# Transformer stage: q/k parts stored one by one and fetched in one transfer of 48 partitions, three head groups normalised early, q's rotation and splitting moved to VectorE

## The reference, cut to what matters

```python
NL, D, H, DFF = (6, 128, 16, 512)   # HD = 8
def _rope(x):      # x1*cos - x2*sin, x1*sin + x2*cos on the two halves of each head
def _attn(q, k, v, mask):
    scores = jnp.einsum('bqhd,bkhd->bhqk', q, k) / np.float32(np.sqrt(HD))
    scores = jnp.where(mask[:, None, None, :], jnp.float32(-jnp.inf), scores)
    w = jax.nn.softmax(scores, axis=-1)
    return jnp.einsum('bhqk,bkhd->bqhd', w, v)
```

## Time and profile before

| | |
|---|---|
| median of 3 runs | 5220.8 us (5213.22 to 5223.22) |
| the profiled execution | 5205.5 us, span 5203.7 us |
| PE busy | 4381.7 us (84%) |
| DVE busy | 3406.6 us (65%) |
| ACT busy | 2302.0 us (44%) |
| POOL busy | 504.0 us (10%) |
| mean granted TensorE clock | 0.879 |

### The profile page before, as it was taken

The page is one execution under the profiler, slowest core; times in us unless marked ns, Lnnn a source line. Parts: engine busy times, 40 slices in busy tenths (PEclk is TensorE's granted clock), DMA queues, the critical chain, the costliest instruction groups (busy, mean ns, idle before and its releaser), DMA issues. The chain is left out here.

```text
span 5203.7 us, 88732 instructions
## 1 busy us (share of the span) xinstructions
PE 4381.7 (84%) x25098; PEld 2768.5 (53%) x25446; DVE 3406.6 (65%) x17506; ACT 2302.0 (44%) x7385; POOL 504.0 (10%) x420
## 2 busy tenths in 40 slices
PE   8999999999999987587787878778733697997979
PEld 6888888888888865223333333333322453333456
DVE  7888888888888876455555555555434594433535
ACT  4555555555555543263545454545422122332313
POOL 0000000000000001111221212222101001222000
PEclk9999999999999988697878787878765698998769
DMA  0000000000000001302222222221100010000001
GB/s 27 2 2 2 2 2 2 2 2 2 2 2 2 2 8 43 51 14 34 38 35 38 34 38 34 37 35 30 18 5 3 14 35 24 9 8 10 19 1 37
DMA packets 89492, 91.41 MB, mean 18 GB/s; under 512 B 21311, under 2 KB 84442, under 8 KB 88811
## 3 DMA queue, kind: packets, MB, share of 16 engines
q1 hardware_dynamic: 89067, 86.46, 8.6%
HBM read 70.22 MB, written 15.39 MB: 16 GB/s over the span
## 5 line engine op out<-in xcount | busy, mean ns | idle before, releaser
L287 DVE CUSTOM_DVE_ANT_0 I-219junk<-I-215encw,I-218expo,I-227rec 128x77 f32<-128x77 f32 x3072 | 941.1, 356 | 5.8
L1307 DVE TENSOR_REDUCE I-41381nmax<-ps 128x1 f32<-128x512 f32 x768 | 498.3, 686 | 235.7 <-PE ps L975 225.6
L1195 ACT ACTIVATE I-41384prob<-ps 128x512 f32<-128x512 f32 x768 | 428.6, 594 | 247.5 <-remote 135.4
L265 ACT ACTIVATE I-217tanh_s<-ps 128x77 f32<-128x77 f32 x1024 | 242.4, 237 | 593.9 <-PE ps L245 593.9
L245 PE MATMUL ps<-I-212hist,I-49small 128*128 128x77 f32 x2048 | 456.5, 304 | 40.6 <-DVE I-212hist L323 40.4
L245 PEld LDWEIGHTS ps<-I-212hist,I-49small 128*128 128x128 f32 x2048 | 304.9, 188 | 296.8 <-DVE I-212hist L323 296.7
L251 PE MATMUL ps<-I-217tanh_s,I-49small 128*128 128x77 f32 x2048 | 454.7, 304 | 0.0
L975 PE MATMUL ps<-I-41375kS,I-41374qS 96*128 96x512 bf16 x768 | 347.4, 479 | 111.4 <-DMA I-41374qS<-parts 53.3
L252 PE MATMUL ps<-I-212hist,I-49small 128*128 128x128 f32 x2048 | 440.0, 297 | 0.0
L247 PE MATMUL ps<-I-212hist,I-216uh_h 128*128 128x128 f32 x2048 | 439.8, 296 | 0.0
L273 ACT ACTIVATE I-223hh<-I-229gate_t,I-228pre,I-222rh 128x1 f32<-128x1 f32 x1024 | 395.5, 386 | 84.6
(11 more groups left out here) (494 smaller groups left out, 7980.0 us busy)
## 6 DMA issues: line engine op xcount, KB each, us to landing
I-41374qS<-parts SPq DMA_DIRECT2D x144, 128.0 KB
parts<-I-41393room SPq DMA_DIRECT2D x36, 384.0 KB, 2.5
I-41375kS<-parts SPq DMA_DIRECT2D x72, 128.0 KB
I-49small<-in_layers SPq DMA_DIRECT2D x6, 768.0 KB, 19.2
I-41374qS<-I-41383mrow SPq DMA_DIRECT2D x192, 2.0 KB
I-41374qS<-I-41390crow SPq DMA_DIRECT2D x192, 2.0 KB
I-41393room<-in_own SPq DMA_DIRECT2D x5, 387.0 KB, 4.0
I-41368wk<-in_own SPq DMA_DIRECT2D x6, 320.0 KB, 12.8
```

Of the source, the lines that this page charges most:

```text
L287: return e.tensor_tensor_reduce(junk[:, 2 * g + b, :], encw[:, g, b, :], expo[:, b, :], inv[:, b:b + 1], rec[:, b, g:g + 1], ALU.mult, ALU ...
L1195: e.activation(prob[:, tau % 2, j, :], k.ps[:, b, :], ACT.Exp, scale=scale).then_inc(free[b], 1)
L1307: e.tensor_reduce(nmax[:, U % HG, i, j:j + 1], k.ps[:, use[0], :], AX.X, ALU.max, negate=True).then_inc(free[use[0]], 1)
```

## The change

1. **Layout.** `qS`, `kS`, `cS` become (partition, batch entry, head, token), so that 16 heads of one entry lie together in a partition. The columns of the k, q, cross-k and cross-q weights are reordered on GpSimd (`by_dim`) from head-major to dimension-major into new tiles `wk_d` and `wq_d`, and `cos` and `sin` are reloaded in that order by 8 DMAs in the setup stage.
2. **Stores and fetch.** The DRAM buffer holds six rows of parts per job. Each part is stored as soon as it is made, in its own DMA, to all the rows that hold it (high 3, middle 2, last 1). One DMA of 48 partitions by 16 KB fetches all six rows. The wait is 48 for stores and 16 for the fetch.
3. **Normalisation.** The sum is taken over groups 0 to 2 only, after which these three are normalised; group 3 gets a reciprocal of its own, of its own `o`. GpSimd multiplies only group 1. The same for the cross attention (`cinv`, `co_in`).
4. **q on VectorE.** `join`, `rest_part` and `last_part` of `q` and `cq` move from GpSimd to VectorE; those of `k` and `ctx` stay.
5. Semaphores of the two halves of `part3` are apart, in SP's stream the jobs `ctx` and `cq` stand ahead of the weight loads, and all tables of `TURNS` are written anew.

```diff
-    vector=("rrrrrrrrmmmmmmmmmmmmmmmmmmmmmmmmmmmmmmmmmmmmm...
+    vector=("rrrrrrrmmmmmmmmmmmmmmmmrmmmmmmrmmmmmmmmmrmmmmm...
...
-        qS = sbuf(ctx, nc, "qS", [ROWS_ALL, NH, B * T], BF16)
+        qS = sbuf(ctx, nc, "qS", [ROWS_ALL, B, NH, T], BF16)
...
-        parts_dram = nc.dram_tensor("parts", (4, 3, P, T), BF16).ap()
+        parts_dram = nc.dram_tensor("parts", (4, 6, P, T), BF16).ap()
...
-                e.wait_ge(s.own, 16 * 2)
+                at = offsets(SMALL)[0]["cos"][0]
+                for d in range(8):
+                    e.dma_start(small[16 * d:16 * d + 16, at:at + 2 * T], small_dram[d:P:8, at:at + 2 * T]).then_inc(s.own, 16)
+                e.wait_ge(s.own, 16 * 10)
...
+        Q_SPOTS = (slice(0, 3), slice(4, 6), slice(3, 4))
+        K_SPOTS = (slice(2, 5), slice(1, 6, 4), slice(0, 1))
...
                             if m == 0 and n == 0:
-                                e.wait_ge(s.jsent3, 96 * (a + 1))
-                                e.wait_ge(s.jsent2, 96 * (a + 1))
+                                e.wait_ge(s.jsent3, 16 * (a + 1))
+                                e.wait_ge(s.jsent2, 16 * (a + 1))
...
                 def attend(a):                                  # vector
-                    e.wait_ge(s.pooled, 3 * (a + 1))
-                    e.reciprocal(inv[:], inv[:]).then_inc(s.inv, 1)
-                    yield
                     for n in range(HG):
                         U = HG * a + n
-                        e.wait_ge(s.inv, a + 1)
+                        if n == 0:
+                            e.wait_ge(s.pooled, 2 * (a + 1))
+                            e.reciprocal(inv[:], inv[:]).then_inc(s.inv, 1)
+                            yield
+                        if n == HG - 1:
+                            e.wait_ge(*done(values(a, n)))
+                            e.wait_ge(s.wide, U)
+                            e.reciprocal(inv[:], o[:, n, :]).then_inc(s.inv, 1)
+                        e.wait_ge(s.inv, 2 * a + 1 + n // (HG - 1))
...
-                        if n % 2 == 0:
+                        if n != 1:
...
                         turn_pair("tx", "txs", 1, T)            # vector; the same behind qx, qxs for "cq"
+                        join("q", "tx", "txs", 1, T)
+                        yield
+                        rest_part("q", 1, T)
+                        yield
+                        last_part("q", 1, T)
                         yield
...
+                    def by_dim(dst, src, ready):                # gpsimd
+                        e.tensor_copy(dst[:, 0:512].rearrange("p (n d h) -> p n d h", n=4, d=8),
+                                      src[:, 0:512].rearrange("p (n h d) -> p n d h", n=4, d=8)).then_inc(ready, 1)
...
-                    def store(name, n, m):                      # sync
+                    def store(name, n, m, which, spots):
                         spot = SPOT[name]
-                        e.wait_ge(s.last, job[r, name])
-                        if times(r, name) > 1:
-                            e.wait_ge(jsent[spot], 96 * (times(r, name) - 1))
-                        e.dma_start(parts_dram[spot, :, :, 0:m].rearrange("r p t -> p r t"),
-                                    part3[:, n, :, 0:m]).then_inc(jstored[spot], 16)
+                        e.wait_ge((jhigh, middle, last)[which][n], job[r, name])
+                        if which == 0 and times(r, name) > 1:
+                            e.wait_ge(jsent[spot], 16 * (times(r, name) - 1))
+                        dst = parts_dram[spot, spots, :, 0:m].rearrange("r p t -> p r t")
+                        e.dma_start(dst, part3[:, n, which, 0:m].unsqueeze(1).to_broadcast(dst.shape)).then_inc(jstored[spot], 16)
 
-                    def spread(name, m, dst, order):
+                    def spread(name, m, dst):
                         spot = SPOT[name]
-                        e.wait_ge(jstored[spot], 16 * times(r, name))
-                        for row, which in enumerate(order):
-                            e.dma_start(dst[8 * row:8 * row + 8, :, c * m:(c + 1) * m],
-                                        parts_dram[spot, which, :, 0:m].rearrange("(h d) t -> d h t", d=8)).then_inc(jsent[spot], 16)
+                        e.wait_ge(jstored[spot], 48 * times(r, name))
+                        e.dma_start(dst[0:ROW_MASK, c, :, :],
+                                    parts_dram[spot, :, :, 0:m].rearrange("r (d h) t -> (r d) h t", h=NH)).then_inc(jsent[spot], 16)
```

More of the change, by code:

```diff
@@ L786, in rest_order, with transformer @@
     return out
-def transformer(nc, k, small, z, ctxT, own_dram, layers, masks, rows, sel_dram):
+def transformer(nc, k, small, z, ctxT, own_dram, layers, masks, rows, small_dram):
     with ExitStack() as ctx:
@@ L858, in _ @@
                     for g in range(HG):
[L859 to L860 removed]
+                        for n in range(HG - 1):
+                            if n != g and g < HG - 1:
                                 e.memset(dst[:, :, 4 * g:4 * g + 4, 8 + n:9 + n], 0.0).then_inc(s.ones, 1)
@@ L1162, in rest @@
                             b = open_bank(e, use)
-                            e.matmul(k.ps[:, b, 0:P], mine[:, i * P:(i + 1) * P], K(4), start=True, stop=True).then_inc(full[b], 1)
+                            e.matmul(k.ps[:, b, 0:P], mine[:, i * P:(i + 1) * P], wk[:, 512:640], start=True, stop=True).then_inc(full[b], 1)
                             yield
```

299 lines of the change are left out of this document (160 added, 139 removed).

## The result

The changed kernel takes **5063.65 us** (median of 4 runs, 5054.96 to 5067.14), the kernel before 5219.66 us in the runs beside it: a ratio of **0.970**, 95% interval 0.9683 to 0.9717, 156 us less. The profiled execution took 5061.74 us (span 5059.6, before 5203.7) at a mean granted clock of 0.889 (before 0.879).

What follows compares the result with a forecast made beforehand. PE was taken to wait for a chain in the gap phase and to be the bound in the score phase. 86.5 + 5 + 17 + 15.5 - 2 = 122 us off 5205.5 gave a forecast of 5098 us, range 5025 to 5175.

Steps and rivals of the forecast that it cites:

- fetch: Transfer of parts on the path to q's landing: one of 48 partitions takes 6 us instead of 12.9.
- first scores, kind of the eighth attention: Gap phase from the eighth attention's last copy to the next first scores: 37 us instead of 55.2.
- the other kind: Gap phase before the eighth attention, from last copy to first scores: 37 us instead of 40.8.
- score phases: From first scores to the attention's last copy, two kinds: 85.5 us becomes 88, 92.6 becomes 91.
- ten rounds: Transformer rounds from first to eleventh reciprocal: 127.5 us each instead of 136.15, gaining 86.5 us.
- round twelve: The transformer's last round, short already: gain 5 us.
- start and setup: Before the rounds: first maxima near 2141 through faster fetch, 17 us gained; two more mask transfers in setup cost 2.
- end: Last cross attention: faster fetch and shorter VectorE chain save 9.5 us, earlier normalisation 6, together 15.5.
- Rival A: The fetch gets no faster (12.9 us), q lands at +16: gain 37 us, 5183 us; chance 0.13.
- Rival B: The gap closes more, projection and cross q at full clock: round 121 us, gain 190, 5030 us; chance 0.17.
- Rival C: In the score phase VectorE's blocks hold up PE: round 147 us, 75 us slower, 5296 us; chance 0.07.
- The lock between VectorE and GpSimd: k's parts beside q's: VectorE operations with two SBUF inputs lock GpSimd out, at most 0.69 us a piece.

Runs made afterwards that it cites:

- x_back: Changed kernel with 33 instead of 22 (once 20) maxima matmuls ahead of the first cross maxima in nine rounds; 5121.1 us, ratio 0.982 to the kernel before.
- x_six: Changed kernel with every fetch of parts again six transfers of 8 partitions instead of one of 48; 5276.4 us, ratio 1.010 to the kernel before.
- x_small: Changed kernel with one fetch of 48 partitions, but DRAM rows 128 bytes apart, so read in pieces of 1 KB; 5081.2 us, ratio 0.975 to the kernel before.
- x_pool: Changed kernel with join, rest and last part of q and cross q back on GpSimd; 5100.0 us, ratio 0.978 to the kernel before.

## Why the prediction was right, point by point

The direction and the range held (5025 to 5175, measured 5063.7), the gain was 156 us for a forecast 122.

| term | forecast | measured |
|---|---|---|
| fetch | 6 | 7.6 (q), 7.9 (k) |
| q lands | +9.3 | +11.1 |
| projection ends | +7.4 | +6.75 |
| layer norm's turn | +11.5 | +12.0 |
| first scores, kind of the eighth attention | +37 | +37.0 |
| the other kind | +37 | +40.7 |
| score phases | 88 and 91 | 84.7 and 82.3 |
| ten rounds | 86.5 gained | 139.6 |
| round twelve | 5 | -0.3 |
| start and setup | 15 | 14.05 |
| end | 15.5 | 11.0 |
| stages behind | 0 | -20.2 |

**The term that was mis-sized is the score phase.** I let the one kind shrink by 1.6 us and the other grow by 2.5; they shrank by 10.3 and 0.8. Over ten rounds, five of each kind, that is 60 us more than forecast; the other kind's gap, 3.7 us longer than forecast, takes 18 of them back, and my taking 127.5 for 126.5 adds 10. Together that is about the 53 us by which the ten rounds beat the forecast.

For the large one I had counted 40 cross maxima leaving, priced as PE's matmul time, 2 us. Before, all 64 and their 16 turns stood in that score phase; now 8 and 8 do. In the two rows above PE's busy time falls by 6.2 and its waiting by 4.1 (10.6 to 6.5). By the groups of lines in these stretches, the cross maxima and turns that left make 3.9 of the 6.2 (4.5 to 1.1 us, 1.5 to 1.0). Clock makes most of the rest: in the trace PE was granted the lower level for 9.4 us of this phase before and for 3.5 now, an estimated 2 to 3 us of busy time. And 2.0 of the 4.1 us of waiting were one wait for cross q's landing (PE L1086 by DMA, at 3106.41), a part of the slow fetch that I had not looked for in the score phase. The other 2 us aren't traced further.

The other kind got 11 maxima, for which I charged 2.5 us in all. x_back prices them at 0.2 each, 2.2 together, so that the charge was about right. What I missed is what the phase loses beside them: PE is busy 1.8 us longer and waits 2.6 us less (9.8 to 7.3), of which 1.2 for exponentials and 0.6 for maxima. Why it waits less no run shows.

**The fetch** was the right cause with a wrong figure. I halved all of 12.9 us (13.2 by the two rows that I named), but only the 11.5 us in flight are halved; 11.5 / 2 + 1.7 gives the 7.4 that the last cross q took. The sum that I made with the Trainium skill ("SBUF — State Buffer", "Door 1: The DMA port swizzle", with a fixed 2 us from "The DMA setup-cost knee") came to an estimated 5.6 us. The fixed part agrees with the 1.7 us here, the 218 GB/s of its eight ports don't: in flight it is 137. Nor does the step from two ports to eight show: the rate grows twofold, 68 to 137, and not fourfold. The rule of the Trainium skill on the number of engines ("DMA: Bandwidth & Descriptors", "Why a DMA increments its semaphore by 16 and not by 1") is borne out by the 8 and 16 steps of the semaphores, and by x_six and x_small: 8 partitions at a time 13.8 us, 48 at a time 8.2 even in pieces of 1 KB.

That the gap came out at 37.0 in spite of it is luck in part. q was 1.8 us late, and my list holds 19 of the 23 maxima ahead of the first scores; against that the projection ran at full clock (2.92 us for three groups, I had 4.9), and the maxima pace the rest.

**Rival A was priced far too low.** I gave it 5183 with q at +16. The chip says 5276 with q at +23: I had overlooked that the new order puts q's stores behind k's fetch on SP's queue, so a slow fetch counts twice. My first maxima at 2141 erred by the same (2151.5, after 19.6 us of waiting): they came 10.6 us sooner and not 21. That start and setup gained 14.05 us for my 15 all the same is luck.

**Rival B** came nearer by its sum (34 + 87 = 121 a round, measured 122.2) but not by its parts: the gap is 39.0 on average and the score phase 83.8. What it said of the projection at full clock came true. Its 190 us were missed by 12 in the ten rounds, by 15 at the edges and by the 20 of the stages behind.

**Rival C** did not come: PE's waits for maxima in the score phases are 0.2 us in one kind and none in the other (before 0.8 and 1.2), and VectorE is busy 57 to 60 of 82 to 85 us.

**The other kind's gap** is 40.7, not 37: there 56 cross maxima, not 40, stand ahead of the first scores. **Round twelve** did not shrink; that it was short already should have made the term 0. **The end** gained 11 for 15.5: the last cross maxima come 34.0 us after the last reciprocal for 44.0, and the early normalisation brings the projection 2.6 us closer to the last product with V (11.0 for 13.6), but those products ran at the lower clock throughout (2.79 us for each eight, where before the last two eights took 2.02 and 2.01).

**The lock between VectorE and GpSimd**, which the prediction named as shown by no row, is in the trace and costs little. In each of ten rounds k's last part on GpSimd starts inside q's join on VectorE:

```profile
3076.47 1.61 POOL L1516 TENSOR_TENSOR I-41395room<-I-41395room 128x512 bf16<-128x512 f32 x1
```

It takes 1.61 us, where x_pool, with q's join on GpSimd, has 1.16. k's last store goes out right behind it, so k's fetch starts an estimated 0.45 us later. In nine of the rounds q's join takes 0.80 us for 0.69.

What stays open: how much of the 20 us behind the transformer belongs to this change. Kernels whose code there is the same differ by as much and more, as the last section shows.

## What to carry to other kernels

Price a change of transfers and a change of order together: the fetch alone was worth 3.9 us a round, the order alone -3.8, and with two cheap edits they made 14. Of a transfer's time halve only the part in flight. On one queue, ask of every store which fetch stands ahead of it. Work that paces the gap is nearly free in the phase where another engine waits in small bits, so count what stands in each phase, exactly and by kind, before giving it a price.
